# The f32 state of a recurrent cell on GpSimd, and its low part behind the other half's cell on VectorE

## The reference

```python
x = x + gnn(layernorm(x), src, dst, weight, bias)      # mean over a node's edges
x = x + lstm(layernorm(x)[None], U_i, V_i, b_i, ..., U_o, V_o, b_o)[0]

def step(carry, xs):
    h, c = carry
    i_t = sigmoid(xi_t + h @ V_i)
    f_t = sigmoid(xf_t + h @ V_f)
    g_t = tanh(xg_t + h @ V_c)
    o_t = sigmoid(xo_t + h @ V_o)
    c_new = h * c + i_t * g_t
    h_new = o_t * tanh(c_new)
    return ((h_new, c_new), h_new)
```

## Time and profile before

| | us |
|---|---|
| median of 3 runs | 496.7 (495.86 to 497.5) |
| the profiled execution | 495.42 |
| its span | 493.6 |
| first `ig` of the full turns starts | 355.69 |
| last `ig` of the full turns starts | 483.54 |

### The profile page before, as it was taken

The page is one execution under the profiler, slowest core; times in us unless marked ns, Lnnn a source line. Parts: engine busy times, 40 slices in busy tenths (PEclk is TensorE's granted clock), DMA queues, the critical chain, the costliest instruction groups (busy, mean ns, idle before and its releaser), DMA issues.

```text
span 493.6 us, 15382 instructions
## 1 busy us (share of the span) xinstructions
PE 420.1 (85%) x6094; PEld 365.6 (74%) x6094; DVE 363.4 (74%) x1157; ACT 345.9 (70%) x894; POOL 173.5 (35%) x313
## 2 busy tenths in 40 slices
PE   2487799978899999999999899997677878999992
PEld 2265577867788888888888788876577777888881
DVE  3869799987788677686776833535577778888884
ACT  1346598456877776777775764556799999999991
POOL 4442600154337345354544523421122222222220
PEclk9999899999999999999999999999999999999996
DMA  8524002320010001000100000000000000110111
GB/s 194 132 52 131 0 2 72 104 90 1 4 51 1 1 1 55 1 1 1 53 2 3 1 22 33 2 1 30 26 3 5 3 3 3 58 35 23 56 56 59
DMA packets 9604, 16.91 MB, mean 34 GB/s; under 512 B 2006, under 2 KB 7451, under 8 KB 9526
## 3 DMA queue, kind: packets, MB, share of 16 engines
q1 hardware_dynamic: 7922, 13.32, 8.7%
q10 hardware_dynamic: 724, 1.67, 1.5%
q0 software_dynamic: 880, 0.86, 0.8%
HBM read 6.23 MB, written 9.61 MB: 32 GB/s over the span
## 4 chain that ended last, share of the span: by engine, by line
DVE 40%; PE 34%; ACT 10%; issue 8%; POOL 6%; DMA 1%; SPq 0%; DVEq 0%; ACTq 0%
PE bank L1144 10%; DVE hots L1489 8%; PE bank L1113 7%; PE bank L1115 7%; ACT tc L946 5%; DVE h L1702 5%; DVE h L1739 5%; DVE c_st L1697 4%; PE bank L1169 3%; DVE h_flat L1702 3%; POOL rstd L658 3%; PE bank L1067 3%; POOL newton L657 2%; PE bank L1097 2%; DVE x_sb L1555 2%
## 5 line engine op out<-in xcount | busy, mean ns | idle before, releaser
L1067 PE MATMUL bank<-hots 128*128 128x125 f16 x625 | 120.6, 220 | 0.2 <-DVE hots L1489 0.2
L1489 DVE TENSOR_TENSOR hots<-iota,kp 128x1024 f16<-128x1024 f16 x157 | 105.6, 701 | 20.0 <-PE bank L1067 17.0
L1236 PE MATMUL bank<-h,V 128*128 128x62 f16 (+1 forms) x2952 | 102.7, 192 | 18.6 <-DVE h L1702 11.1
L1236 PEld LDWEIGHTS bank<-h,V 128*128 128x128 f16 x2952 | 94.9, 97 | 29.6 <-issue 28.0
L1113 PE MATMUL bank<-h_flat,counts 125*128 125x257 f16 x375 | 97.3, 273 | 0.2 <-ACT counts L799 0.2
L1115 PE MATMUL bank<-h_flat,counts 125*128 125x256 f16 x375 | 96.4, 271 | 0.0
L657 POOL TENSOR_SCALAR newton<-rstd,var_eps 125x1 f32<-125x1 f32 x48 | 33.6, 701 | 116.9 <-DVE rstd L1561 114.5
L799 ACT ACTIVATE counts<-bank 125x500 f16<-125x500 f32 x96 | 55.4, 607 | 20.5 <-PE bank L1067 19.0
L1113 PE MATMUL bank<-h_flat,gx 125*128 125x257 f16 x250 | 68.2, 273 | 0.0
L691 POOL TENSOR_TENSOR hc<-h_flat,c_st 128x126 f32<-128x126 f32 x80 | 34.1, 426 | 96.6 <-DVE c_st L1697 91.7
L1115 PE MATMUL bank<-h_flat,gx 125*128 125x256 f16 x250 | 67.4, 270 | 0.0
(11 more groups left out here) (171 smaller groups left out, 795.1 us busy)
## 6 DMA issues: line engine op xcount, KB each, us to landing
h_dram<-h_flat SPq DMA_DIRECT2D x1, 3137.2 KB
x_dram<-x_sb SPq DMA_DIRECT2D x5, 625.0 KB
out_dram<-x_sb SPq DMA_DIRECT2D x4, 560.0 KB
x_sb<-in_x_dram SPq DMA_DIRECT2D x3, 560.0 KB
x_sb<-in_x_dram ACTq DMA_DIRECT2D x2, 560.0 KB
out_dram<-x_sb SPq DMA_DIRECT2D x1, 336.0 KB
out_dram<-x_sb SPq DMA_DIRECT2D x4, 65.0 KB
gx<-in_L_gnn_weight_dram ACTq DMA_DIRECT2D x1, 256.0 KB, 3.8
```

The lines of the kernel that those rows point to most:

```text
L1067: nc.tensor.matmul(ps_count[group % 3][:, pos * KEYS:(pos + 1) * KEYS], hots[:, ring, 0, g // 2, :, g % 2], hots[:, ring, 1, g // 2, 0:KEY ...
L1236: mm = nc.tensor.matmul(to[:, (m - m0) * n:(m - m0 + 1) * n], V16[:, v_part, d, m * P:(m + 1) * P], h16[:, h_part, d, c0:c1], start=False, ...
L1489: nc.vector.tensor_tensor(hots[:, k % RING, :, :, :, :].rearrange("p a h n g -> p (a h) n g"), iota[:, :, :].unsqueeze(1).to_broadcast(of) ...
```

## The change

The change takes the f32 state of a full turn from VectorE and computes it on GpSimd, in two instructions: `go1` is the gate of o plus one (it needs only the gate), and its product with the cell's tanh is the state. `go1` lies in memory that the one-hot tiles (`hots`) used earlier. GpSimd's order in a half turn is then `go1`, state, `hc`, all of the same half, and `hc` waits for that half's own cell and state. At turn 40 and at turn 65 VectorE keeps writing the f32 state itself.

On VectorE the low part of the other half moves from before the cell to behind it.

```diff
+        go1 = hots[:, 0, ...].rearrange(...)[:, 0:4 * HH * n_half].bitcast(F32).rearrange(
+            "p (q m k) -> p q m k", q=2, m=HH)
...
+            def exact_state(q, t):
+                c0, c1 = COLS[q]
+                n = c1 - c0
+                raised[q] += 1
+                pool.wait_ge(o_gate[q], t - HIDDEN)
+                nc.gpsimd.tensor_scalar(go1[:, q, :, 0:n], gate[:, q, 2 * HH:MT, 0:n], 1.0, None, ALU.add
+                                        ).then_inc(o_raised[q], 1)
+                pool.wait_ge(o_raised[q], raised[q])
+                pool.wait_ge(tc_ready[q], t - HIDDEN)
+                nc.gpsimd.tensor_tensor(h_after(t)[:, :, c0:c1], go1[:, q, :, 0:n], tc[:, q, :, 0:n], ALU.mult
+                                        ).then_inc(h_ready[q], 1)
...
                 for q in range(2):
-                    if n - 1 + q > 0:
-                        pool.wait_ge(c_ready[1 - q], n - 1 + q)
-                    if n > 1:
-                        pool.wait_ge(h_ready[q], n - 1)
-                    old_part(q, h_before(t), c_before(t))
+                    if n == 1:
+                        old_part(q, h_before(t), c_before(t))
+                for q in range(2):
+                    if t == DONE:
+                        continue
+                    if not ends_round(t):
+                        exact_state(q, t)
+                    pool.wait_ge(c_ready[q], n)
+                    pool.wait_ge(h_ready[q], n)
+                    old_part(q, h_before(t + 1), c_before(t + 1))
...
                 if not ends_round(t):
                     state(q, h16[:, 0, :, c0:c1], n).then_inc(hi_ready[q], 1)
-                    state(q, h[:, :, c0:c1], n).then_inc(h_ready[q], 1)
                     return
...
                     new_part(q, n)
+                    cell_after(q)
                     if q == 0 and n > 1:
                         state_low(1, t - 1)
                     elif q == 1 and t < DONE:
                         state_low(0, t)
-                    cell_after(q)
```

More of the change, by code:

```diff
@@ L211, in bass_gnn_lstm_kernel @@
         tc = sb("tc", [P, 2, HH, n_half])
+        go1 = hots[:, 0, :, :, :, :].rearrange("p a h n g -> p (a h n g)")[:, 0:4 * HH * n_half].bitcast(F32).rearrange(
+            "p (q m k) -> p q m k", q=2, m=HH)
         def whole(t, m):
@@ L339, in bass_gnn_lstm_kernel @@
         hi_ready = [sem(f"hi_ready{i}") for i in range(2)]
+        o_raised = [sem(f"o_raised{i}") for i in range(2)]
         lo_ready = [sem(f"lo_ready{i}") for i in range(2)]
@@ L692, in old_part @@
                                         ).then_inc(hc_ready[q], 1)
+            raised = [0, 0]
+            def exact_state(q, t):
[9 more added lines that the diff above has]
+                                        ).then_inc(h_ready[q], 1)
             pool.wait_ge(e_h, HIDDEN - SHARP + 2)
```

## The result

The changed kernel takes 532.8 us (median of 4 runs, 531.56 to 533.74), the kernel before 497.1 in the runs beside it: the ratio is 1.071, 95% interval 1.069 to 1.074. It is 35.7 us slower. The prediction was 541, its range 517 to 563; the direction and most of the size came as forecast. One term of 19 us had the wrong instruction, and by luck 9 us of a term that the sum lacked stand in its place: without them the miss of 8 us would have been twice as large.

A forecast was written before the change was run, and what follows sets the result against it. Two balanced loops of 1.57 us per half turn were taken as the bound. Order 25.6 plus held cell 19.2 gave 44.8 us over the profiled 495.42, so 540.2; 1.3 more for the median gave 541, range 517 to 563.

The forecast's parts named there:

- One term of 19 us: Full turns: VectorE's cell held by GpSimd's `go1`, 0.24 us in each of 80 half turns, 19.2 us.
- Two loops of 1.57: Full turns: one half's high part to high part, and low part, gate, `ig`, other half's low part; both 1.57 us.
- a step in front of the low part is paid in full: VectorE: the cell ahead of the low part lengthens the half-to-half loop by 0.32 us, 25.6 us in all.
- the loop of one half: High part, TensorE, gate, `ig`, cell, tanh, next high part: 3.13 us a turn, 1.57 per half turn.
- The f32 state taken off VectorE: 0: Removing VectorE's 0.28 us state behind each high part only gives VectorE idle time; the turn gains 0.
- GpSimd fits: GpSimd's three operations with their signal delays need 1.53 us of a 1.89 us half turn.
- The held cell, 0.24: VectorE's cell stands still while GpSimd runs `go1`, ending 0.24 us later per half turn, low part included.
- The cell isn't held: Rival: VectorE's cell runs free beside `go1`, only the order counts, 522 us; chance 0.25.
- GpSimd as the bound by its own work: Rival: GpSimd's operations, stretched by VectorE's, bring half a turn near 2.4 us, 563 us in all; chance 0.15.
- a hidden part: Rival: about 0.15 of slack in the 0.79 from low part to gate, no holding, 510 us; chance 0.05.
- a gain: Rival: the first loop sets the pace at 1.53 us, 3 us less, 493.5 us; chance 0.03.
- the clock: TensorE's granted clock might drop as its work falls to 59% from 80%; no chance of its own.

The follow-up runs named there:

- e1: Kernel before, with only the low part moved behind the cell, f32 state still on VectorE: 522.8 us against 497.5, ratio 1.050.
- e7: Kernel before, with TensorE's four high products for the gate of o moved behind the low products of i and g: 497.3 us against 497.4, ratio 1.000.
- e3: Changed kernel, with `hc` of a half moved behind the next half's `go1`: 527.5 us, ratio 1.061.
- e6: As e3, but `go1` adds one to twice as many elements, half of the result unused: 536.0 us, ratio 1.077.
- e4: Changed kernel, with `go1` adding a tile of ones (two inputs) instead of a constant: 541.9 us, ratio 1.090.
- e2: Changed kernel, with the low part back ahead of the cell, so only the f32 state goes to GpSimd: 512.9 us, ratio 1.031.
- e5: As e2, but VectorE computes `go1` while waiting for tanh; GpSimd keeps the state's product and `hc`: 511.9 us, ratio 1.030.

## Why the prediction was right, and where it wasn't

- **Two loops of 1.57; a step in front of the low part is paid in full.** The second half is right: e1 lengthens the way to the low part by 0.32 and pays 25.3 us, where the sum had 25.6. In e1 the parts are 0.32, 0.20, 0.79 and 0.57. Of the first half e7 shows that the loop of one half isn't needed. The tanh ahead of the gate, to which the prediction gave "a few hundredths", makes a loop of the whole 1.57 (see e7).
- **The f32 state taken off VectorE: 0.** Right as far as the rows go. In e1 `ig` waits 0.40 to 0.42 for its gate, in the changed kernel 0.60 to 0.62: the 0.20 that VectorE is rid of turned into idle time. No run takes the state away alone.
- **GpSimd fits.** Right for its busy time: 1.45 of 2.01, and it waits for tanh in 74 places. Go1 is 0.55 at the median, a little over the upper bound (0.53) and not the 0.47 taken; it isn't on the loop that sets the pace. The state's product is 0.49, not 0.41, and it is on that loop.
- **The held cell, 0.24.** This is the step that failed. It placed go1 and the cell rightly (go1 at 0.24 behind `ig`, as in the trace) and applied to go1 a hold that the trace had shown for `hc`, an instruction with two inputs. Go1 has one. e3 and e6 show what that is worth: 0.05 to 0.07 at this size. e4 gives go1 a second input and gets the held cell.
- **`hc` beside `ig`, 0.11.** The prediction left it out. It followed `hc` only for when its result is wanted, and never asked what VectorE does while it runs. With its own sizes the hold would have cost nothing (told here without the held cell, which moves all of them alike): tanh ends 0.98 behind `ig`, and with 0.08 ahead of the state and of `hc` and 0.41 for each, `hc` ends at 1.96 and a held `ig` at 2.11, while a free `ig` that starts at 1.89 ends at 2.18. Measured, the state starts 0.15 behind tanh's end and `hc` 0.62 behind the state. That moves `hc` over the next `ig` and closes the loop of 2.00. `ig` takes 0.40 at the median instead of 0.29, and 80 x 0.11 = 9 us stand where the sum had 19.
- **Which VectorE work is held.** SCALAR_TENSOR_TENSOR is: started behind a two-input GpSimd instruction of this size, it ends 0.14 to 0.15 behind that one's end (e2, e4, e5). So the exclusive lock that the Trainium skill states ("SBUF — State Buffer", section "SBUF: two separate sides") agrees for that form; for one-input go1 the hold ends before the instruction does (e6), and there the measurement decides. Nor does go1 run near line rate, as the Trainium skill's "GPSIMD Engine Reference", section 4.1, has it for one-input work: 0.55 for 126 elements and 0.84 for 252, where VectorE needs 0.21 for the same sum of 126 (e5).
- **The rivals.** "The cell isn't held" was right about the cell (0.29; the prediction had named 0.28 as its sign) and gave 522, since it left out `ig` too. GpSimd as the bound by its own work, a hidden part, a gain and the clock did not come.

## What to carry to other kernels

Before moving an instruction, write down every loop that closes in one period, not only the longest idle time, and count the order on each engine among its links: a gate that stands behind a tanh closes a loop too. Shortening one of several loops of equal length gains nothing (e7); lengthening one is paid in full (e1). When work goes to GpSimd, lay each of its instructions with two inputs over VectorE's row. In this kernel a SCALAR_TENSOR_TENSOR that started beneath one ended 0.15 us behind it, and that can tie together parts of the program that share no data.

## What the runs showed of the hardware

- How GpSimd holds VectorE depends on the form of its instruction. A TENSOR_TENSOR of 126 elements on GpSimd (0.40 to 0.47) stretches a SCALAR_TENSOR_TENSOR from 0.29 up to 0.49; a TENSOR_SCALAR of 0.52 stretches it by 0.05, one of 0.84 by 0.16 (e3, e6).
- It goes the other way too: the state's product, started 0.12 behind VectorE's high part, takes 0.49 instead of the 0.41 of `hc` when nothing runs beside it. In e6 the same product, begun once (391.79) when the high part had 0.08 left, takes 0.41.
- Who comes first matters at a few hundredths: in e2 the low part, 0.08 ahead of `hc`, takes its plain 0.28, while `hc` takes 0.47 and the cell, 0.12 behind `hc`, 0.49.
- A shorter GpSimd instruction can be the dearer one: 0.46 with two inputs costs 9 us more than 0.55 with one (e4).
